# GpSimd folds half of each whole batch, in the second half of the batches, before ScalarE sums it

## The reference, cut to what matters

```python
scores = clip(q @ k.T / sqrt(HD), -50, 50);  scores = where(attend, scores, -10000.0);  scores = clip(scores, -50, 50)
probs = softmax(scores);  ctx = probs @ v;  delta = rs * (ctx @ Wo.T + bo)
x = x + tanh(g_xattn) * layernorm(delta)
x = x + tanh(g_ffn) * moe(layernorm(x))          # softmax over 8 experts, the best 2
```

## Time and profile before

| | |
|---|---|
| median of 3 runs | 290.21 us (290.14 to 292.1) |
| the profiled execution | 291.79 us, span on the core 290.10 us |
| mean granted TensorE clock | 0.927 |
| sums of whole batches, ScalarE (L802) | 24 of 128x1500, 35.1 us, and 4.8 us to read the accumulators |
| sums of whole batches, VectorE (L1021) | 8, 13.6 us |

### The profile page before, as it was taken

One profiled execution on the slowest core, in us unless ns is written; L12 is line 12 of the kernel. 1 busy time (PEld: TensorE's weight loads), 2 busy tenths in 40 slices (PEclk: granted clock), 3 DMA queues, 4 the chain that ended last, 5 costly groups with the idle time before them and its releaser, 6 DMA issues.

```text
span 290.1 us, 7184 instructions
## 1 busy us (share of the span) xinstructions
PE 236.3 (81%) x2704; PEld 181.2 (62%) x2704; DVE 179.2 (62%) x415; ACT 137.8 (48%) x220; POOL 62.5 (22%) x102
## 2 busy tenths in 40 slices
PE   0619389999999999859998629399899567999994
PEld 0309268888888888638886529296575336565653
DVE  7677805458899963365298923446379991494535
ACT  5135723567688678854378870220523406620110
POOL 2820021124245111101033200000625246210000
PEclk9999959999999999985999976859999997999998
DMA  7325801296798999988523000030000000020002
GB/s 177 90 54 162 353 5 39 67 329 239 274 292 325 341 385 427 398 260 316 214 83 137 2 0 2 3 64 5 0 0 0 0 0 2 0 63 1 2 0 64
DMA packets 12871, 37.55 MB, mean 129 GB/s; under 512 B 2321, under 2 KB 10017, under 8 KB 10529
## 3 DMA queue, kind: packets, MB, share of 16 engines
q1 hardware_dynamic: 12016, 36.65, 36.8%
q10 hardware_dynamic: 720, 0.40, 0.6%
q0 software_dynamic: 96, 0.00, 0.0%
HBM read 35.14 MB, written 0.92 MB: 124 GB/s over the span
## 4 chain that ended last, share of the span: by engine, by line
PE 56%; issue 19%; ACT 11%; DVE 7%; POOL 5%; DVEq 1%; POOLq 0%; ACTq 0%
PE bank L484 11%; PE bank L491 9%; PE bank L689 8%; PE bank L501 8%; PE bank L512 6%; PE bank L706 5%; ACT ctx_all L802 5%; ACT p L790 4%; POOL x_sb L461 4%; PE bank L476 3%; PE bank L593 1%; PE bank L469 1%; ACT normed L806 1%; PE bank L583 1%; DVE p L1171 1%
## 5 line engine op out<-in xcount | busy, mean ns | idle before, releaser
L790 ACT ACTIVATE p<-bank,mask_bias,mask_scale 125x896 f32<-125x896 f32 x38 | 39.6, 1093 | 43.8 <-PE bank L501 43.8
L484 PE MATMUL bank<-ctx_pair,wk 128*128 128x250 f32 x152 | 40.4, 410 | 5.9 <-issue 5.9
L689 PE MATMUL bank<-rowsT,gate_up 128*128 128x448 f32 x112 | 44.6, 541 | 0.0
L388 POOL COPY q_slot<-qbd 128x224 f32 x38 | 17.1, 453 | 95.2 <-PE bank L501 67.0
L491 PE MATMUL bank<-wv,ctx_pair 128*125 128x256 f32 x152 | 36.9, 387 | 0.0
L1002 DVE TENSOR_SCALAR p<-p 125x912 f32<-125x912 f32 x38 | 28.1, 754 | 14.1 <-ACT p L790 14.1
L484 PEld LDWEIGHTS bank<-ctx_pair,wk 128*128 128x128 f32 x152 | 29.1, 202 | 12.1 <-issue 7.0
L706 PE MATMUL bank<-down,act 128*112 128x256 f32 x128 | 31.8, 393 | 4.5 <-DVE act L1260 3.6
L802 ACT ACTIVATE ctx_all<-ctx_all 128x1500 f32<-128x1500 f32 x24 | 35.1, 1467 | 0.0
L491 PEld LDWEIGHTS bank<-wv,ctx_pair 128*125 128x125 f32 x152 | 29.3, 193 | 4.6
L706 PEld LDWEIGHTS bank<-down,act 128*112 128x112 f32 x128 | 23.1, 184 | 13.8 <-DVE act L1260 4.7
(11 more groups left out here) (147 smaller groups left out, 295.2 us busy)
## 6 DMA issues: line engine op xcount, KB each, us to landing
ctx_all<-ctx_dram SPq DMA_DIRECT2D x16, 1500.0 KB, 6.8
ctx_pair<-ctx_dram SPq DMA_DIRECT2D x38, 125.0 KB, 5.0
gate_up<-gate_up_dram SPq DMA_DIRECT2D x1, 2048.0 KB, 10.0
down<-down_dram SPq DMA_DIRECT2D x1, 1024.0 KB, 11.9
num<-acc SPq DMA_DIRECT2D x16, 57.0 KB, 2.7
x_sb<-x_dram SPq DMA_DIRECT2D x2, 448.0 KB, 6.4
out_dram<-x_sb SPq DMA_DIRECT2D x4, 224.0 KB, 2.4
wq<-wq_dram ACTq DMA_DIRECT2D x1, 256.0 KB, 4.4
```

The costliest lines, as they stand in the source:

```text
L388: nc.gpsimd.tensor_copy(targets[t], source).then_inc(flow.q_in, 1)
L484: mm = nc.tensor.matmul(bank[:, K_BANK, 2 * TT * m:2 * TT * (m + 1)], wk[:, k, P * m:P * (m + 1)], tile[:, :, k, :], start=(k == 0), stop= ...
L689: mm = nc.tensor.matmul(bank[:, GU_BANK[s % 2] + g, 0:HR], gate_up[:, e, k, g, :], rowsT[:, k, HR * h:HR * (h + 1)], start=(k == 0), stop= ...
L790: nc.scalar.activation(p_tile[:, t].rearrange("t (j n) s -> t j n s", j=4)[:, :, :, 0:S], bank[0:TT, 0:4, DEN * t:DEN * (t + 1)].rearrange ...
```

## The change

GpSimd gets one more instruction per batch from batch 8 on, after the query copies (and the guess, if there is one) of pair b + 6: it adds tiles 6 to 11 of `ctx_all` onto tiles 0 to 5, both halves at once, 128x1500 values from two places in SBUF. It waits for the load of the batch and counts up a new semaphore `folded`. ScalarE's sums of batches 8 to 15 wait for that instead of the load, and each reads 6 tiles, 750 values. Batches 0 to 7 stay as they are, and so do all other instructions and their order.

```diff
@@ -48,6 +48,7 @@
+FOLD = NT // 2
@@ -161,6 +162,7 @@
+        folded = sem("folded")
@@ -415,6 +417,12 @@
+            def fold(b):
+                pool.wait_ge(all_in[b % STREAMS], 16 * (b // STREAMS + 1))
+                low, high = (ctx_all[b % STREAMS][:, FOLD * f:FOLD * (f + 1)].rearrange("p n k t -> p (n k t)")
+                             for f in range(2))
+                nc.gpsimd.tensor_tensor(low, low, high, ALU.add).then_inc(folded, 1)
+
@@ -441,6 +449,8 @@
                 if i == 20:
                     h_guess(0)
+                if i - NOPT >= HB:
+                    fold(i - NOPT)
@@ -797,8 +807,12 @@
             def sum_all(b, k):
-                act_e.wait_ge(all_in[b % STREAMS], 16 * (b // STREAMS + 1))
-                mine = ctx_all[b % STREAMS][:, :, k, :]
+                if b < HB:
+                    act_e.wait_ge(all_in[b % STREAMS], 16 * (b // STREAMS + 1))
+                    mine = ctx_all[b % STREAMS][:, :, k, :]
+                else:
+                    act_e.wait_ge(folded, b - HB + 1)
+                    mine = ctx_all[b % STREAMS][:, 0:FOLD, k, :]
                 nc.scalar.activation(mine, mine, ACT.Identity, accum_out=total[:, k, b:b + 1]).then_inc(
```

## The result

| | before | after |
|---|---|---|
| median (runs) | 290.17 us (4) | 296.80 us (4) |
| lowest to highest | 288.06 to 292.1 | 295.52 to 298.01 |
| the profiled execution, and its span | 291.79, 290.1 | 297.22, 295.5 |
| mean granted TensorE clock | 0.927 | 0.924 |

The ratio is 1.0229, with a 95% interval of 1.0145 to 1.0314: the change makes the kernel 6.6 us slower. The forecast was 300.1 us (+9.9), with a range of 293.5 to 303.0. The direction and the mechanism held. The size was 3.3 us too large.

What follows compares the result with a forecast made beforehand. TensorE was busiest (81%), with ScalarE's sums and the `den` wait on the chain. Holds put the v copy 12.8 us late, transposes 10.5; 0.6 for low clock, minus 1.25 for sums: +9.9 on 290.21, so 300.1 us, range 293.5 to 303.

Steps and rivals of the forecast that it cites:

- rival A: All holds of VectorE by folds as laid out: 300.1 us, own range 298.0 to 302.5, chance 0.52.
- rival B: One hold missed: 296.7 us if the small chain precedes fold 15, 297.0 if fold 11 misses `den`; chance 0.25.
- D: Folds don't hold VectorE, so the kernel gets faster: 287.8 us, chance 0.07.
- E: Only the `den` hold reaches the path, the rest falls into VectorE's slack: 290.9 us, chance 0.08.
- C: Two holds are missed: about 293.5 us, chance 0.08.
- The fold: GpSimd's addition of 128x1500 values from two SBUF inputs: 3.4 us each.
- Batches 8 to 10: Folds before `den` lands hold clips and delay sums, but slack and the `den` wait cover it: cost 0.
- Batch 11: Fold running when `den` lands holds `den_less` and `den_sum`, shifting the spread matmul: +3.1 us (2.4 to 4.0).
- Batch 12: Fold holds `totals(0)` to about 136, where VectorE has slack: 0 (up to 1 us).
- Batch 13: Fold right behind `delta_guess(0)` holds `half_var`, plus two copies: +2.9 us on VectorE (2.4 to 3.2).
- Batches 14 and 15: Folds behind `h_guess(0)` hold `half_var`, then a late small instruction of the chain to `offset`: +3.4 us each.
- The slow stretch behind the wait: Pair 21: `v_proj` at the low clock, 3.3 us instead of 1.89; transposes and `pv` add 0.6.

Runs made afterwards that it cites:

- hold_only: Kernel before plus an addition of 112x1500 on unused memory at each fold's place, ScalarE summing all 1500 values: 297.12 us, ratio 1.0405.
- sums_only: Changed kernel without folds, ScalarE summing only the lower six tiles of batches 8 to 15 after the load: 284.52 us, ratio 0.9922.
- no_fold14_15: Changed kernel without the folds of batches 14 and 15, whose sums read 1500 values: 290.38 us, ratio 1.0125.
- placed: Changed kernel with only folds 13, 14 and 15: before `delta_guess(0)`, behind it, and behind the v copy of pair 20: 283.48 us, ratio 0.9797.
- placed_again: The kernel with only folds 13, 14 and 15 at places of VectorE's slack, run once more: 286.04 us, ratio 0.9935.
- no_fold11: Changed kernel without the fold of batch 11, whose sums read 1500 values: 292.08 us, too scattered for a ratio.
- late15: Changed kernel with fold 15 waiting for VectorE's v copy of pair 20: 294.81 us, ratio 1.0201.

## Why the forecast was right, and where it was too large

**The mechanism, rival A: right, but by the rows and not by the total.** 296.8 us lies below A's own range (298.0 to 302.5) and on rival B's 296.7, one hold missed; what speaks for A is that every hold of the sum is there, each with its fold beside it. `hold_only` and `sums_only` show that the holds alone make the loss and that the sums save little; rivals D and E fall, and B and C didn't happen in the changed kernel. B's case was met in `no_fold14_15`, and there it was not worth the 3.1 us that B gave it: the hold only moved to the next instructions.

**The fold: right.** 3.4 us forecast, 3394 ns on average. The Trainium skill (GPSIMD Engine Reference, section 3.1) gives 4497 ns for 2048 values, by which 1500 would be an estimated 3.29 us; the trace agrees to about 3%.

**Batches 8 to 10: right, 0.** The clip of pair 13 was held 3 us (3.70 at 103.64), fold 9 came at 115.80 where 115.7 was forecast, and ScalarE waited 2.93 us for it without any effect behind the `den` wait.

**Batch 11: right mechanism, +2.65 for +3.1.** The forecast put two query copies of 0.3 us between; `den_sum`, VectorE's instruction, got in first (128.70). **Batch 12: right, 0.** `masked_less` was held 2.78 us, and `delta_guess(0)` was 2.79 late, hardly more than the spread's 2.65.

**Batch 13: +2.4 for +2.9.** `half_var` takes 2.40 for 0.16, and the copies behind it lengthen the next small instructions by 0.18 in all, where the forecast had 0.68. **Batches 14 and 15: +6.57 for +6.8.** From `h_guess(0)` to the v copy the delay grows from 5.19 to 11.76. `half_var` takes 3.31, 2.7 more than before and not 3.4, since before already had 0.63 instead of 0.16 there, beside its own query copies. `newton` takes 4.02, 3.9 more and not 3.4: what fold 15 caught was not one of the late instructions of the chain, as forecast, but the second, held from its start over both copies and the fold. That the two nearly add up to the forecast is in part luck. Together: v copy 11.76 late for 12.8 forecast.

**The slow stretch behind the wait: the term that was mis-sized.** The forecast had `v_proj` at the low clock, 3.3 us, let the low clock go on through the transposes and `pair_pv` for 0.6 more, and had no term for the scores. `v_proj` took 3.78. The transposes began 9.76 late for 10.5 and took 0.94 for 0.57. But then `pair_pv` took 1.00 and the scores 1.14 us, where before had 1.50 and 2.04. The granted clock of the changed kernel (stretch; length; busy us of PE, PEld, DVE, ACT and POOL; then the clock, DMA share and GB/s):

```profile
170.00:176.00 6.00, 5.01 (x57) 3.90 (x60) 5.37 (x14) 1.81 (x4) 0.00 (x0) 0.55 0.00 0
176.00:182.00 6.00, 1.64 (x70) 1.40 (x57) 4.23 (x12) 4.15 (x7) 1.56 (x1) 1.00 0.01 3
```

So the scores began 9.63 us late (176.36 against 166.73) and, 0.90 us shorter, ended 8.73 late, for the 11.1 forecast. The step that failed is "they and `pv` at the low clock add 0.6": from the start of the transposes to the end of the scores the delay didn't grow by 0.6, it shrank by 1.03. The low clock lay on `v_proj` and the transposes and was over before `pair_pv`, and `pair_pv` and the scores were the work that had been slow before, behind the wait of 2.56 us. The forecast had no row for how far the low clock reaches.

**The sums: right.** 1.25 us forecast; 8.73 - 7.48 = 1.25.

**Behind pair 21** the forecast let the delay stand. It shrank from 7.48 to 6.87 and then to 5.44 us. From 240 to 250 a place is visible: the transposes of the second half take 0.57 us at 247.71 and the eight matmuls behind them 1.89, where before has 0.98 at 240.84 and 3.13. The change touches nothing there, so I put it down to how the clock's stretches fell in these two executions. From `masked_sums(1)` to the last silu nine of the fourteen profiles take 105.6 to 106.1 us and five 107.3 to 108.6. Before (108.12) is one of the five, the changed kernel is both times among the nine, and one and the same kernel stands on either side (`placed` 105.76, `placed_again` 107.33). So some 2 us of the difference between the two profiled executions are probably not the change's. In these profiles the way from the forecast's 9.85 to the 5.44 is: 0.74 ahead of the transposes, 1.63 from there to the scores' end, 2.04 behind `masked_sums(1)`. The medians are 6.6 us apart; how the 3.3 us that are missing from the forecast split among these isn't settled.

**Adding up parts.** Alone, folds 14 and 15 cost 1.4% in one group; without them the rest costs 1.25% in another. With 290 us that is 3.9 + 3.6 = 7.5 us, near the 6.6 of the whole, though the rest had its first hold moved. Where TensorE's clock falls differs from profile to profile (`no_fold11`, `placed`), so the totals of such parts don't measure a hold; the local lines do.

## What to carry to other kernels

Before work goes to an idle GpSimd, list VectorE's small instructions that wait for a GpSimd result or a DMA at that point in time: a long GpSimd instruction queued right behind the one they wait for catches them for its whole length or longer, and cutting it into four didn't help here. If the work is worth moving, put it behind a wait that says that VectorE's chain is done. And where a new wait brings TensorE's low clock, ask which work it will lie on and which it leaves free: work that was slow before may now be fast.

## What the runs showed that I had not expected

- GpSimd instructions that stand ready back to back keep a held VectorE instruction out over several of them: two copies and a fold, 0.68 + 3.34 = 4.02 us; four pieces of a fold, 3.74; two copies and four pieces, 4.44. The 4.02 stands, to 0.01 us, in four profiles of three kernels. The copies alone don't do it: beside them and with no fold behind, the same `newton` took 0.15 us (`late15` at 167.85). Why the fold behind reaches back over the copies, and why it didn't in `hold_only`, stays open. The Trainium skill (SBUF — State Buffer, "Who interferes with whom") calls the shared ports an exclusive lock. The trace agrees on the exclusion; by it a hold would end with the instruction that it met, and in these rows it goes on.
- An accumulation that reads PSUM and one SBUF input ran in its free 0.40 us in the midst of fold 13 (154.39), and a v copy in its free 0.67 beside fold 12 (132.20). So what the forecast allowed for these, up to 1 us, didn't arise. A `fix_raw` from PSUM ran free too (0.74 at 158.99), beside fold 15 of `placed`. Beside folds 13 and 15 of these two kernels `half_var` and the pass after `fix_raw`, each with one SBUF input and an SBUF output, were held.
- An addition of 1500 values whose two inputs are the same stretch took 2.68 us (`hold_only`, on 112 partitions), and 3.38 with two different ones (on 128). I didn't test whether the partitions matter.
- A slow stretch of TensorE can cost nothing by its place: in `no_fold11` the low clock followed a wait of 2.97 us that ended at 122.6, and so lay in the time in which `den` was awaited anyway, and the pair behind it ran at the full clock.
